# Row maxima of the rounded attention scores: one PSUM bank per reduce instead of two neighbouring banks

## What is computed

```python
scores = jnp.einsum('bhqd,bhkd->bhqk', q, k) / math.sqrt(hd)
causal = jnp.triu(jnp.ones((S, S), dtype=bool), k=1)
scores = jnp.where(causal[None, None], -jnp.inf, scores)
attn = jax.nn.softmax(scores, axis=-1)
attn_out = jnp.einsum('bhqk,bhkd->bhqd', attn, v)
```

## Time and profile before

| | |
|---|---|
| median of 3 runs | 1687.47 us (1686.44 to 1688.21) |
| the profiled execution's own time | 1689.95 us |
| its span, first to last instruction | 1688.2 us |
| PE busy | 1601.0 us, 95% |
| DVE busy | 953.0 us, 56% |
| ACT busy | 723.3 us, 43% |
| POOL busy | 670.2 us, 40% |
| mean granted TensorE clock | 0.972 |

### The profile page before, as it was taken

The page is one execution under the profiler, slowest core; times in us unless marked ns, Lnnn a source line. Parts: engine busy times, 40 slices in busy tenths (PEclk is TensorE's granted clock), DMA queues, the critical chain, the costliest instruction groups (busy, mean ns, idle before and its releaser), DMA issues.

```text
span 1688.2 us, 47262 instructions
## 1 busy us (share of the span) xinstructions
PE 1601.0 (95%) x20500; PEld 1168.5 (69%) x20500; DVE 953.0 (56%) x1977; ACT 723.3 (43%) x1526; POOL 670.2 (40%) x851
## 2 busy tenths in 40 slices
PE   6799999999999999999999999999999999999998
PEld 3476468865788557884588756886478855787477
DVE  6865657257663657446663565636565365734621
ACT  5443462335632564234633346323552246333342
POOL 5734335243532426334362434424353342723110
PEclk9898999989999999999999999998999989999799
DMA  5210000000000000000000000000000000000000
GB/s 178 64 51 13 14 2 3 0 26 14 3 2 13 14 14 3 1 26 2 15 3 1 26 15 3 2 1 26 15 3 2 13 14 2 3 1 1 2 13 13
DMA packets 20414, 26.21 MB, mean 16 GB/s; under 512 B 1489, under 2 KB 18801, under 8 KB 20209
## 3 DMA queue, kind: packets, MB, share of 16 engines
q1 hardware_dynamic: 19872, 22.15, 3.9%
q0 software_dynamic: 336, 1.05, 0.2%
HBM read 19.00 MB, written 4.19 MB: 14 GB/s over the span
## 4 chain that ended last, share of the span: by engine, by line
PE 81%; DVE 8%; issue 3%; ACT 2%; POOL 1%; DVEq 0%; POOLq 0%; ACTq 0%
PE ring L1642 20%; PE ring L1656 18%; PE ring L1588 7%; PE ring L1628 6%; PE ring L1810 5%; PE attn_out L1837 5%; PE ring L1761 4%; PE ring L1695 3%; DVE maxes L1383 2%; PE ring L1783 2%; PE ring L1580 2%; PE ring L1665 1%; PE ring L1789 1%; DVE big L1316 1%; PE ring L1845 1%
## 5 line engine op out<-in xcount | busy, mean ns | idle before, releaser
L1383 DVE TENSOR_REDUCE maxes<-ring 128x2 f32<-128x256 f32 (+6 forms) x289 | 197.9, 742 | 94.0 <-PE ring L1789 93.3
L804 POOL TENSOR_TENSOR rstd<-mean_var,eps_and_power 128x2 f32<-128x2 f32 x96 | 19.5, 203 | 450.6 <-DVE mean_var L1219 450.5
L1656 PE MATMUL ring<-w_down,big 128*128 128x256 f32 x784 | 176.7, 379 | 0.0
L856 POOL TENSOR_TENSOR big<-big,decay_blocks 128x256 f32<-128x256 f32 x192 | 140.8, 761 | 53.2 <-issue 48.6
L1656 PEld LDWEIGHTS ring<-w_down,big 128*128 128x128 f32 x784 | 147.2, 190 | 19.6 <-issue 0.4
L1073 ACT ACTIVATE big<-ring,up_bias 128x256 f32<-128x256 f32 x196 | 82.3, 471 | 135.4 <-PE ring L1642 135.4
L1316 DVE TENSOR_TENSOR big<-big,decay_blocks 128x256 f32<-128x256 f32 x192 | 124.2, 673 | 1.0
L827 POOL TENSOR_TENSOR mix<-mix,z_t 128x512 f32<-128x512 f32 x80 | 86.6, 1107 | 93.7 <-DVE mix L1271 93.6
L1810 PE MATMUL ring<-big 32*64 32x128 f32 (+3 forms) x2048 | 118.0, 492 | 3.6 <-DVE big L1415 1.5
L1642 PE MATMUL ring<-maxes,w_mlp 128*128 128x256 f32 x512 | 118.4, 385 | 1.2 <-issue 1.2
L1642 PE MATMUL ring<-maxes,w_up 128*128 128x256 f32 x512 | 117.7, 381 | 0.7 <-ACT maxes L1004 0.7
(11 more groups left out here) (202 smaller groups left out, 3262.2 us busy)
## 6 DMA issues: line engine op xcount, KB each, us to landing
x_in<-in_x SPq DMA_DIRECT2D x8, 512.0 KB, 3.7
delta<-in_x SPq DMA_DIRECT2D x7, 512.0 KB, 3.9
out<-x_z_xb SPq DMA_DIRECT2D x7, 512.0 KB, 2.8
w_mlp<-in_wm SPq DMA_DIRECT2D x2, 1024.0 KB, 6.3
w_mlp<-in_w_exp_t SPq DMA_DIRECT2D x1, 1028.0 KB, 8.9
v_ones<-in_w_con SPq DMA_DIRECT2D x1, 1024.0 KB, 9.8
w_mlp<-in_low_up SPq DMA_DIRECT2D x1, 1016.0 KB, 5.9
w_attention<-in_low_down SPq DMA_DIRECT2D x1, 1016.0 KB, 7.7
```

Of the source, the lines that this page charges most:

```text
L856: nc.gpsimd.tensor_tensor(kv, kv, dv.unsqueeze(2).to_broadcast([P, T // (2 * s), s]), ALU.mult).then_inc(*one(kg_level))
L1383: nc.vector.tensor_reduce(maxes[:, t % 2, qt, 32 * gs[0] + row:32 * gs[-1] + row + 1:32], banks[:, first:last, lo:hi], AX_X, ALU.max).then ...
L1656: ins = mm(ps[:, a * D:(a + 1) * D], gelu(b, tag, m, t)[:, a * P:(a + 1) * P], wd[:, m, :], start=(m == 0), stop=(m == NF - 1))
```

## The change

`runs` closes a run after one bank, so that every reduce takes the columns of one bank.

```diff
-                if found and found[-1][1] == i - 1 and len(found[-1][2]) < 2:
+                if found and found[-1][1] == i - 1 and len(found[-1][2]) < 1:
```

## The result

The changed kernel takes 1690.91 us, the kernel before on the same chip 1685.92 (medians of 22 runs each): ratio **1.0032, interval [1.0017, 1.0046]**; 0.32% of 1686 is 5.4 us (the medians themselves differ by 5.0). The ratio is taken without the executions that took far longer than all others, one of the kernel before (8528 us) and two of the changed one (1849 and 3371 us). A second comparison gave 1.0032 again. The forecast of 2.6 us, 0.15%, had the direction; the size is twice as large, and with it the change is slower by more than the 0.2% that the likeliest case allowed (the interval reaches down to 0.17%).

A forecast was written before the change was run, and what follows sets the result against it. PE bounds the kernel, DVE time counting only where PE waits for it. Terms 0.2 + 0.9 + 0.65 + 0.8 = 2.6 us, added to the median 1687.47, give 1690.1 us; range 1685.5 to 1696.5.

The forecast's parts named there:

- the likeliest case: Whole kernel: 0 to 3.4 us slower, time between 1687.5 and 1691 us; chance 0.50.
- The added reduce: DVE, rounds a to c: each added reduce costs 0.06 to 0.075 us, taken as 0.065, since durations overlap.
- The early start of 0.11 us: Where the DVE stands waiting for PE, a round's first reduce no longer waits for a second bank: 0.11 us earlier.
- Turn 3: Round c at turns 2 and 3: two more reduces, 0.13, less the early start 0.11, so +0.02 us per turn.
- turn 0: Rounds a and b at turn 0: the turn comes 0.15 us later in most batches, 0.9 us over batches 0 to 6.
- PE's added waits: 164 more PE instructions carry a wait: taken as nothing, with 1.6 us as the upper bound.
- An added reduce costs its whole fixed part: Rival, all turns: without overlap each added reduce costs 0.147 us, 11 us in all, 1698.5 us; chance 0.09.
- faster: Rival: early starts count (3.5 us), added reduces do not, and PE's 2.1 us of bank waits go: 1681.9 us; chance 0.07.
- Turn 1: Round c at turn 1 starts as before and ends 0.13 us later in five of batches 0 to 6: 0.65 us.
- Against: 0.15 us is little: Argument against more clock falls between turns 0 and 1: idle time grows only 0.15 us, and a fall less is possible.
- its last term, 0.8 us for the last batch: Last batch, less other work beside it: added reduces delay two turns by 0.28 us each and one by 0.2.
- The rival: PE's longer idle at turn 0 makes the clock fall more often: 3.6 us per fall, 1693.7 or 1697.3 us; chance 0.14.

The follow-up runs named there:

- the two halves of the change: Against the kernel before: single banks only in rounds a and b of t = 0, 1.0035; single banks everywhere but there, 0.9993.
- the repeated reduce: Kernel before with the last reduce of round b of t = 0 made a second time, the turn waiting for it: 1.0043.
- the filler at turn 0: Kernel before with six useless identity matmuls on PE before turn 0, results overwritten: 0.9930, 1674.52 us against 1687.13.
- the same filler at turn 3: Kernel before with the six useless products before the turn of t = 3 instead of t = 0: 1.0022.
- Splitting unevenly: Kernel before with the first head's bank reduced alone and the other three in one reduce where the ring allows it: 1.0060.

## Why the prediction was half right

**Right.** The added reduce costs 0.065 us and not 0.147: eight of round b take 2.72 to 2.74 us (2.75 forecast), four of round c 1.42 (1.42 forecast). The early start of 0.11 us is there. Turn 3 is mostly 0.02 to 0.03 us later after its mask (forecast 0.02), turn 2 of batches 1 to 6 not at all (1.75 us in both kernels), turn 0 is 0.15 later (forecast 0.15) in batches 1, 3, 4 and 5, the windows from turn 1 to 2 grow by 0.02 us, PE's added waits cost nothing measurable. PE's wait at L1845 grew by 3.8 us, where some 2 were forecast. "An added reduce costs its whole fixed part" and "faster" are both out.

**Mis-sized, two terms.** Turn 1: 0.13 was forecast, 0.02 came. The step said that round c "follows other DVE work" once the 0.26 us are used up and so starts when it did before. It starts 0.06 us after the mask instead of 0.16: the early start was to be had there as well, since the added reduces of round b fill the idle time exactly and no more. I had counted the delay of round b and left out the gain of round c. With that the term is 0.1 us instead of 0.65. DVE busy: 32 us was the sum of durations; the page's figure counts overlap once, so 12.9.

**The step that failed** is the one that costs the clock at nothing: "Against: 0.15 us is little". With turn 1 put right the direct terms are 0.2 + 0.9 + 0.1 + 0.8 = 2.0 us. The runs allow 0 to 1.6 us at equal clock, so this sum is at the upper end or too high; its last term, 0.8 us for the last batch, no run bears out. The other part of the 5.4 us, 4 us or more, comes with a mean granted clock that is lower by 0.004 to 0.005. The rival named the place (turn 0, ahead of the fall), its price (3.6 us for one more fall) and its sign, and got 0.14. It should have had about half. It also had the push too small: "that idle time grows by 0.15" counts the later turn alone, and the profile shows 0.38 us more (1.20 for 0.82), since the banks that come back singly take away the wait ahead of L1618 and PE stands at the turn instead. The prediction had said of these waits that they may go but that "the turn behind waits for the same reduces"; it did not carry this over to the idle time of the rival. The rows for that stood in the profile: of six like batches four fell and two did not, and PE's idle time at turn 0 was 0.82 us in batch 1, which fell, and in batch 4, which did not. Where the outcome is so evenly split, a small push moves it; that it had not fallen in two batches was no sign of a margin.

What is shown and what is not: that the loss sits in rounds a and b of t = 0 is shown by the two halves of the change; that a later turn 0 lowers the clock, by the repeated reduce (0.9694 against 0.9730); that PE's idle time there is what does it, by the filler at turn 0 against the same filler at turn 3. Not shown is how much of the change's own effect comes from the 0.15 us by which the turn is later and how much from the 0.23 us of pause that moved to it. The split of the time into a direct part and a part of the clock rests on slopes that scatter from 850 to 1330 us per unit. That the time came out inside the range owes something to luck: 0.65 us for turn 1 and up to 0.8 us for the last batch were in the sum and are not borne out, and they stood in for a part of the clock's loss, which was not in it. Why one batch falls in one execution and not in the next is open. The last batch can't be separated: turns 0 and 1 come 0.9 and 0.8 us later after their masks there, where 0.2 to 0.3 were forecast, but its clock is low in both kernels.

## What to carry to other kernels

Splitting a reduce so that it starts on its first operand bought about 0.1 us per start and cost 0.065 us per added instruction; so split only the round in which the start counts, and count the instructions that follow in the same run of work. Splitting unevenly has a third price, the buffers that come back late. Where the granted clock falls in some of several like stretches and not in others, look at what PE does ahead of them, and treat a few tenths of a microsecond added to its idle time there as a change of the odds of a fall. Count in what an earlier bank does: a short wait that goes away ahead of a fixed one makes that one longer. And try a filler: a few products into a bank that is overwritten anyway, ahead of the wait. Here that is worth more (12.6 us) than anything the width of the reduces can give; the fastest kernels of this study are the ones with such products, pairs or single banks alike (0.9930 and 0.9931). How few of them do, and whether fewer that don't overrun would give the rest, was not tried.

## What the runs showed of the hardware

- An idle time of PE of 0.82 to 1.38 us at turn 0 is followed in 33 of 42 batches of the table (the seven kernels without filler at turn 0) by a stretch at 1.2 GHz that costs up to 3.6 us; 1.4 to 2.3 us of useless products in its place keep the clock at 2.4 GHz in all 18. The Trainium skill describes a case like it on the page "TensorE: Matmul & The Clock Gate", section "A second HAM failure mode: psum-queue depth-cycling": short idles of PE between groups of matmuls can make the clock swing between its two levels. The trace agrees, with 0.75 to 0.83 in the windows above against 1.00 with filler.
- In rounds b and c a reduce that waits for two banks starts 0.13 to 0.16 us after the last mask product, one that waits for a single bank 0.03 to 0.06 us. In some rounds a, where the reduce is 512 columns of a bank, the two are 0.17 and 0.11 us.
- Reduces from PSUM of one form after another overlap: eight with durations of 548 and 279 ns in turn, 3.31 us by their sum, take 2.72 us.
